# SyncE fetches no blocks of rows, and GpSimd's gathers wait for each pair of blocks

## What is computed

```
xn  = layernorm(x)
h   = xn @ W
deg = segment_sum(edge_weight, dst) + 1;  dinv = rsqrt(deg)
agg = segment_sum((dinv[src] * edge_weight * dinv[dst])[:, None] * h[src], dst)
agg = agg + (dinv * dinv)[:, None] * h
gnn = relu(0.5 * (layernorm(agg + b) * gamma + beta) + 0.5 * xn)
x   = x + gnn + linear_attention(xn)
x   = x + moe(layernorm(x))
```

## Time and profile before

| | us |
|---|---|
| median of 3 runs | 2265.05 |
| lowest, highest | 2261.67, 2266.09 |
| profiled execution, span | 2246.5 |
| its edge stage (first gather with a wait to the last gather) | 258 to 1672 |
| TensorE busy in the span | 1583.4 (70%) |
| VectorE busy | 1134.0 (50%) |
| GpSimd busy | 1042.0 (46%) |

### The profile page before, as it was taken

How to read it: one execution, slowest core, us unless ns; L and a number is a source line. 1 busy time by engine, 2 the same in 40 slices (tenths; PEclk the granted TensorE clock), 3 DMA queues, 4 the chain that set the end, 5 groups by cost and what they waited for, 6 DMA issues and landing times. The chain is left out here.

```text
span 2246.5 us, 37994 instructions
## 1 busy us (share of the span) xinstructions
PE 1583.4 (70%) x7988; PEld 1272.2 (57%) x7989; DVE 1134.0 (50%) x4097; ACT 486.3 (22%) x1376; POOL 1042.0 (46%) x1093
## 2 busy tenths in 40 slices
PE   8998355576556666665567655475756899999997
PEld 5676344455445445444445444354544699998885
DVE  8997233443334444443444333443446655556559
ACT  4444110111101111110111110111102444444434
POOL 1323455544445545444544545454540355554556
PEclk9999676777777777777777776777777999999999
DMA  6106222222222222222222222222225522224338
GB/s 224 38 30 159 72 76 69 74 60 71 68 66 73 71 68 71 67 75 66 75 62 69 73 71 71 71 70 58 79 71 116 158 82 91 91 90 157 119 112 305
DMA packets 131263, 201.58 MB, mean 90 GB/s; under 512 B 49798, under 2 KB 86028, under 8 KB 131180
## 3 DMA queue, kind: packets, MB, share of 16 engines
q0 software_dynamic: 47952, 131.12, 20.0%
q1 hardware_dynamic: 82940, 68.92, 10.3%
q10 hardware_dynamic: 288, 0.66, 0.1%
HBM read 166.97 MB, written 34.39 MB: 90 GB/s over the span
## 5 line engine op out<-in xcount | busy, mean ns | idle before, releaser
L135 POOL DMA_INDIRECT ring<-table,src x776 | 736.8, 950 | 750.3 <-PE bank L1153 418.9
L1153 PE MATMUL bank<-ring,late_hots 128*128 x384 | 156.3, 573 | 361.9 <-SPq L814 232.8
L1153 PE MATMUL bank<-ring,hots 128*128 x1372 | 340.7, 406 | 94.5 <-remote 70.9
L1153 PEld LDWEIGHTS bank<-ring,hots 128*128 128x128 f32 x1372 | 279.4, 206 | 148.7 <-issue 106.0
L1153 PEld LDWEIGHTS bank<-ring,late_hots 128*128 128x128 f32 x384 | 105.0, 287 | 405.7 <-issue 387.9
L1091 ACT ACTIVATE xn<-x,half_s,half_r (+1 forms) x48 | 28.8, 600 | 1071.5 <-PE bank L1244 450.0
L1686 PEld LDWEIGHTS bank<-one,w 128*128 128x128 f32 x1696 | 205.0, 192 | 10.1 <-issue 3.8
L1686 PE MATMUL bank<-one,w 128*128 128x128 f32 x1696 | 207.4, 275 | 1.6 <-issue 1.1
L1694 PE MATMUL bank<-w,one 128*128 128x256 f32 x848 | 203.0, 381 | 6.2 <-DVE y L1758 4.7
L1659 ACT ACTIVATE one<-bank,b 128x128 f32<-128x128 f32 x424 | 142.8, 366 | 232.5 <-PE bank L1686 203.5
L1605 POOL DMA_INDIRECT spread<-y,to_x x109 | 108.2, 993 | 169.2 <-DVE y L1758 75.4
(11 more groups left out here) (294 smaller groups left out, 2507.0 us busy)
## 6 DMA issues: line engine op xcount, KB each, us to landing
w<-in_w SPq DMA_DIRECT2D x32, 512.0 KB
ring<-table,src POOLq DMA_INDIRECT x776
side<-table SPq DMA_DIRECT2D x768, 1.0 KB
got<-spread SPq DMA_DIRECT2D x11, 1024.0 KB, 9.7
rows<-xn SPq DMA_DIRECT2D x1, 6272.0 KB, 25.4
out<-xn SPq DMA_DIRECT2D x12, 512.0 KB, 5.8
xt<-in_x_cols SPq DMA_DIRECT2D x11, 512.0 KB, 3.5
table<-xn SPq DMA_DIRECT2D x5, 896.0 KB, 6.3
```

Of the source, the lines that this page charges most:

```text
L135: return pool.indirect_dma_start(out=m.ring[:, b % RING, :], out_offset=None, in_=a.table, in_offset=bass.IndirectOffsetOnAxis(ap=m.src[:, ...
L1153: last = nc.tensor.matmul(agg, hot[:, k, :], two[:, k, :], start=False, stop=False)
```

## The change

SyncE's fetches, their index lists and their two DRAM buffers go; what is left of its work in `layers` is the relays, each waiting for its four landings. GpSimd gathers all 782 blocks. Its wait for `freed` stands before every second block and asks for the one pair whose slots the next two gathers take.

```diff
-ROWS_EVERY = 116
-BY_ROWS = [ROWS_EVERY * (k + 1) + 38 for k in range(6)]
...
-            for k, b in enumerate(BY_ROWS):
-                sp.dma_start(a.row_src[k][:, None], m.src[:, b:b + 1]).then_inc(picked, 16)
-            sp.wait_ge(picked, 16 * len(BY_ROWS))
...
-            def relay(step):
-                sp.wait_ge(landed[step % 8], by_pool(step) * 16)
-                for k, b in enumerate(BY_ROWS):
-                    if b // 4 == step:
-                        sp.wait_ge(side_in, k * 16 + 16)
+            for step in range(FULL // 4):
+                sp.wait_ge(landed[step % 8], (step // 8 + 1) * 64)
                 sp.sem_inc(gathered, 2)
-
-            def fetch_row(k, r):
-                row = sp.value_load(row_src[0:1, r:r + 1])
-                row = nc.s_assert_within(row, 0, NP - 1, skip_runtime_bounds_check_because="an index of a row of x")
-                sp.dma_start(a.side[k, r:r + 1], a.table[bass.ds(row, 1)]).then_inc(row_in, 16)
-
-            def send_block(k):
-                b = BY_ROWS[k]
-                sp.wait_ge(freed, (b + 2 - RING) // 2 + CREDIT)
-                sp.dma_start(ring[:, b % RING, :], a.side[k]).then_inc(side_in, 16)
...
             for b in range(GATHERED_AHEAD, FULL):
-                if b in BY_ROWS:
-                    continue
-                if b >= RING and b % 4 == 0:
-                    pool.wait_ge(freed, (min(b + 4, FULL) - RING) // 2 + CREDIT)
+                if b >= RING and b % 2 == 0:
+                    pool.wait_ge(freed, (b + 2 - RING) // 2 + CREDIT)
                 gather(pool, m, a, b).then_inc(landed[b % RING // 4], 16)
```

More of the change, by code:

```diff
@@ L700, in layers @@
         mark = sb("mark", [P, 1])
-        row_src = sb("row_src", [1, P], I32)
         score = sb("score_l", [P, E])
@@ L718, in layers @@
             "chain", "chain_rs", "chain_h", "chain_x1", "chain_top", "both_ok", "turn_ok", "start_ok"))
-        picked, row_in, side_in = map(sem, ("picked", "row_in", "side_in"))
         moments_ok, momtr_ok, momT_ok, ctx_ok, ctxT_ok, attend_mm = map(sem, (
@@ L798, in _ @@
                 sp.wait_ge(rg.again, 16 * GATHERED_AHEAD)
-            for k, b in enumerate(BY_ROWS):
-                sp.dma_start(a.row_src[k][:, None], m.src[:, b:b + 1]).then_inc(picked, 16)
-            sp.wait_ge(picked, 16 * len(BY_ROWS))
[L802 to L807, removed]
-            def relay(step):
-                sp.wait_ge(landed[step % 8], by_pool(step) * 16)
-                for k, b in enumerate(BY_ROWS):
-                    if b // 4 == step:
-                        sp.wait_ge(side_in, k * 16 + 16)
-                sp.sem_inc(gathered, 2)
@@ L826, in _ @@
[L826 to L843, removed]
+            for step in range(FULL // 4):
+                sp.wait_ge(landed[step % 8], (step // 8 + 1) * 64)
+                sp.sem_inc(gathered, 2)
             for k in range(FULL % 4 // 2):
-                sp.wait_ge(landed[FULL % RING // 4], by_pool(FULL // 4 - 8) * 16 + 32 * (k + 1))
+                sp.wait_ge(landed[FULL % RING // 4], FULL // RING * 64 + 32 * (k + 1))
@@ L1996 @@
     a.edges = nc.dram_tensor("edges", (NEP, 3), F32).ap()
-    a.side = nc.dram_tensor("side", (len(BY_ROWS), P, D), F32).ap()
-    a.row_src = nc.dram_tensor("row_src_d", (len(BY_ROWS), P), I32).ap()
     a.rows = nc.dram_tensor("rows", (NP, D + 2), F32).ap()
```

## The result

The changed kernel takes **2125.8 us** (median of 4 runs, 2117.4 to 2135.6) where the kernel before takes 2265.6 us (2261.7 to 2273.0): a ratio of **0.938, with a 95% interval of 0.934 to 0.942**. The forecast was 2141 us.

A forecast was written before the change was run, and what follows sets the result against it. The edge stage was bound by GpSimd and TensorE waiting for each other, with SyncE's relays late behind row fetches. -119 + 1 - 6 = -124 us gave a span of 2122.5, plus 18.5 a median of 2141 us; 8-in-10 range 2068 to 2222.

The forecast's parts named there:

- The relay and the row fetches bound the end of a tile: Edge stage: SyncE's relays queue behind row fetches; without them 43 tiles take 27.7 us each, 1191 against 1310 us: -119 us.
- the fetch-free stretch: Old trace from 1568.3 us on, without row fetches; three periods of 26.7, 27.2 and 28.0 us modelled the changed kernel.
- Six more gathers: GpSimd takes over SyncE's six blocks: five already counted in the tiles, the sixth +1 us; 7.5 us in all.
- The finer wait: GpSimd's wait for one freed pair before two gathers: 12 late restarts come one 0.86 us visit earlier, taken as -6 us.
- moving two gathers from the start of a burst to the end of the last is worth nothing: GpSimd's bursts under the new wait: two gathers shift to the previous burst's end, worth nothing, the tile's number stays.
- The sum: All terms on the span: -119 + 1 - 6 = -124 us, from 2246.5 to 2122.5 us.
- Where GpSimd's idle time would stay: GpSimd between its last gather and its next burst: the idle 8 us of each tile was to stay.
- the sign of a wrong step: The forecast would be wrong if the chain from a burst's end to the next start took over 9 us.
- Rival A: GpSimd's bursts split into 14 and 2, the chain overlaps: periods of 26 us and less, below 2070 us; chance 0.07.
- Rival B: TensorE's late pairs also await other late signals: 2215 to 2260 us, chance 0.07, or in full 2266 us, 0.04.
- Rival C: Unbroken GpSimd bursts hold up TensorE's last pairs until the burst ends: up to +60 us, 2325 us; chance 0.09.
- The 18.5 us over the span: Whole kernel: the median stood 18.5 us over the profiled span and was kept so, making 2122.5 into 2141 us.

The follow-up runs named there:

- e12: The changed kernel (no row fetches on SyncE) with the old wait for two pairs before four gathers; held condition, 2088.0 us, 0.930 of the kernel before.
- e6: The changed kernel itself, unaltered, run again on another chip beside the kernel before; held condition, 2126.7 us, ratio 0.940.
- e2: The kernel before, fetches kept, with only the wait changed to one pair before two gathers; free condition, 1729.9 us, ratio 1.001.

## Why the prediction was right, and where not

- *The relay and the row fetches bound the end of a tile* (-119 us). The mechanism was right: the wait for SyncE went, the late pairs follow the early ones at once, and the whole changed kernel has the period of 27.7 us that the fetch-free stretch had given. But the size belongs to both edits together. Leaving out the fetches alone gives 43 x (30.5 - 26.6) = 168 us by the trace of e12, 7.0% or 158 us by its ratio, against 118 with the six gathers in the forecast. The step that failed is the model: I took the three fetch-free periods for those of any kernel without fetches, with 8.2 us between an unbroken burst and the next. In e12 these are 6.9 us.
- *Six more gathers* (+1 us in the stretch, 7.5 in all). The 7.5 us are right where GpSimd sets the pace, in the free condition: 7 to 9 us, 1.005, in four comparisons. The +1 us of the held condition was not seen alone.
- *The finer wait* (-6 us). Wrong in sign in the held condition: a loss of 18 us by the nearest ratios (23 with e6). The restart does come earlier, as forecast: 1.3 and 1.9 us after the first visit in the two traces of the changed kernel, 2.2 in e12 (medians). In 29 bursts GpSimd then stops after 14 blocks for a `freed` that comes some 3 us after the last of them, and the period has two stops for one. The step "moving two gathers from the start of a burst to the end of the last is worth nothing" may have failed there, but in e6 only 19 bursts do so and the time is nearly the same. What failed in both is the price, one visit for each restart that comes one visit earlier: what follows the start took longer, and TensorE spent 425 and 276 us idle in L1093 against 36. Why is open.
- *The sum* (-124 us). By the ratios it is some 158 us of gain and 18 of loss, where the forecast had 118 and a gain of 6. The two errors, 40 and 24 us, point opposite ways, and that they nearly cancel was luck.
- *Where GpSimd's idle time would stay* ("8 us"). The sum of both stops in the tile shown is 8.1 us, but from the end of the 14 gathers to the next start it is 10.3, over the 9 us that I had named as the sign of a wrong step. The sign was right to look at.
- *Rival A*, the split 14 and 2 with periods below 26, got its split in 29 bursts but not its gain: the two late gathers lie in the chain's time, yet the chain is longer. *Rival B* is out, for L1105's late matmuls wait for nothing. *Rival C* held the right suspicion, that the two gathers moved would cost, with the wrong mechanism: the visits are through 6.5 us into the burst in the tiles shown of both kernels, and a tile with an unbroken burst is not the longer one (26.6 against 27.5 us, and 27.4 against 27.7 in e6).
- *The 18.5 us over the span.* Not a constant of the kernel but the distance of one short execution from the median; around the span lie 1.9 us. The gain was priced in that short execution, and taken off a median some 17 us above it: 124 us, where the two spans differ by 117 and the medians by 140. That accounts for the 15 us by which the forecast of the median was too long.
- What the profile of before could not tell is that another condition exists, in which the same change costs 9 us instead of bringing 140.

## What to carry to other kernels

A stretch of the old trace in which the cause is absent is a good model for the time without it, but only for the other edits as they were in that stretch; an edit that moves where a burst stops needs its own model. Where an engine issues DMAs in bursts, try the coarser wait too, beside the finer one: without the fetches, the wait that is never stricter brought nothing in the free condition (1.005 and 1.005) and the higher ratio in the held one (0.938 against 0.930). And time the kernel before beside each variant, for its own time may jump by a quarter with nothing changed.

## What the runs showed of the hardware

**The hold-up by gather bursts comes and goes.** The same kernel on the same data took 2250 to 2266 us or 1729 us. The whole difference lies in and behind the stage of gathers (last gather 1671.5 against 1181.3 us in e2, which differs from the kernel before in the wait only; that is 490 of the 520 us between the spans). In the held condition small instructions of the sequencers take some 700 ns again and again, signals arrive after the burst, and TensorE's granted clock is 0.74 in the stage, with its work spread out; the free one shows none of it, and 0.87. Both are means over stretches at 1.2 and at 2.4 GHz. The clock of the stage in the changed kernel and in e2 (length, busy of PE, PEld, DVE, ACT, POOL, PEclk, DMA share, GB/s):

```profile
256.60:1531.90 1275.30, 835.52 (x3399) 642.13 (x3398) 562.65 (x2327) 157.60 (x453) 697.22 (x734) 0.74 0.26 76
```

```profile
230.00:1180.00 950.00, 809.48 (x3538) 633.92 (x3539) 589.52 (x2417) 166.78 (x465) 720.02 (x755) 0.87 0.38 107
```

A TensorE at 0.87 instead of 0.74 does not make the difference: its busy time is 836 and 809 us in these stretches, which differ by 325 us, and the waits are what goes. What sets the condition is open. It is not the kernel and not the chip alone.

**In a held burst the others are not stopped but go through one by one**, on TensorE with 1.1 to 2.4 us idle before each instruction, and how far they get before the burst ends decides what is left for the pause. In the tiles shown the hold-up starts some 9 us into the burst in the changed kernel and some 11 us in e12; why, no run shows. That the gathers cause it is read from where the slow instructions lie; in the free condition the same gathers at the same pace cause nothing, so they are at most one of two causes.

**The gathers themselves never slowed**: 940 to 1319 ns with a median of 946 to 949 in every kernel and both conditions, VectorE busy beside them in all. The starvation of descriptors of a GpSimd-issued DMA that the Trainium skill states (SBUF — State Buffer, "SBUF: two separate sides") is not in any of these traces, the held ones included; VectorE's costliest operations beside the gathers take 0.35 to 0.48 us in the mean, and a long copy was not tried.

**What stays open**: what makes a group of runs held or free; why the finer wait costs time when held, and how much, for it never ran beside e12's kernel; whether the instructions or the DMAs of the fetches delayed the relay in the held condition; what the finer wait alone, and a pause, would do there. No kernel tried is shown to beat the one before in both conditions: without the fetches and with the old wait it is the fastest when held (2088 us), and with the fetches it is the fastest when free (1729 us).
